# Query and key projections ordered by dimension and then head, so that a stack row is one 16 KB run in DRAM

## What is computed

```
q = _split_heads(query @ Wq.T + bq, B, S)
k = _split_heads(key @ Wk.T + bk, B, S)
v = _split_heads(value @ Wv.T + bv, B, S)
scores = jnp.einsum('bhqd,bhkd->bhqk', q, k) / jnp.sqrt(jnp.float32(D_K))
scores = jnp.where(m == 0, jnp.float32(NEG), scores)
p_attn = jax.nn.softmax(scores, axis=-1)
x = jnp.einsum('bhqk,bhkd->bhqd', p_attn, v)
```

## Time and profile before

| | us |
|---|---|
| median of 3 runs | 1913.74 |
| lowest and highest | 1909.86 and 1918.1 |
| the profiled execution, its own time | 1915.38 |
| its span, first to last instruction | 1913.6 |
| PE busy | 1609.9 (84%) |
| DVE busy | 1219.6 (64%) |
| ACT busy | 1094.1 (57%) |
| POOL busy | 771.6 (40%) |
| mean granted clock of TensorE | 0.929 |

### The profile page before, as it was taken

One profiled execution on the slowest core, in us unless ns is written; L12 is line 12 of the kernel. 1 busy time (PEld: TensorE's weight loads), 2 busy tenths in 40 slices (PEclk: granted clock), 3 DMA queues, 4 the chain that ended last, 5 costly groups with the idle time before them and its releaser, 6 DMA issues.

```text
span 1913.6 us, 34724 instructions
## 1 busy us (share of the span) xinstructions
PE 1609.9 (84%) x10422; PEld 1188.9 (62%) x10422; DVE 1219.6 (64%) x3300; ACT 1094.1 (57%) x2418; POOL 771.6 (40%) x962
## 2 busy tenths in 40 slices
PE   5942778999999899999999889989999899999764
PEld 4731556666666666666666566666666666666542
DVE  5854255676677667766676667666766676676533
ACT  1210235666666666665666666666666566666653
POOL 2335333444444344443444344443444444444221
PEclk9965788999999999998999999999999999999876
DMA  8711333333223212232333332322222233322200
GB/s 269 225 26 44 84 73 73 74 79 80 73 75 79 70 51 72 73 74 71 79 79 80 80 79 79 77 72 65 75 72 62 62 74 79 79 79 63 52 13 11
DMA packets 148988, 147.25 MB, mean 77 GB/s; under 512 B 10930, under 2 KB 147772, under 8 KB 148540
## 3 DMA queue, kind: packets, MB, share of 16 engines
q1 hardware_dynamic: 148796, 144.92, 29.1%
HBM read 99.79 MB, written 42.99 MB: 75 GB/s over the span
## 4 chain that ended last, share of the span: by engine, by line
PE 35%; issue 20%; DVE 14%; DMA 12%; POOL 9%; SPq 6%; ACT 4%; DVEq 0%; POOLq 0%; ACTq 0%
PE bank L1381 15%; DMA qs<-qsplit_d 9%; PE bank L1302 6%; PE bank L1275 4%; PE bank L1264 3%; PE bank L1249 3%; DVE hm L1084 2%; SPq L527 2%; SPq L543 2%; POOL pl L661 2%; DMA qsplit_d<-pl 2%; POOL hid L640 2%; DVE mx L1036 2%; POOL x L656 2%; DVE bn L854 1%
## 5 line engine op out<-in xcount | busy, mean ns | idle before, releaser
L786 ACT ACTIVATE pt<-bank 128x512 f32<-128x512 f32 x512 | 302.2, 590 | 257.4 <-PE bank L1249 257.2
L1036 DVE TENSOR_REDUCE mx<-bank 128x2 f32<-128x512 f32 x512 | 334.6, 683 | 80.4 <-PE bank L1302 80.0
L635 POOL TENSOR_TENSOR x<-x,et 128x256 f32<-128x256 f32 x256 | 190.1, 743 | 329.6 <-ACT et L820 329.4
L1302 PE MATMUL bank<-ks,qs 96*128 96x256 f32 x1024 | 231.6, 311 | 76.2 <-DMA qs<-qsplit_d 59.6
L1302 PEld LDWEIGHTS bank<-ks,qs 96*128 96x128 f32 x1024 | 174.8, 200 | 153.0 <-issue 63.5
L640 POOL TENSOR_TENSOR hid<-hid,t 128x256 f32<-128x256 f32 x256 | 187.1, 731 | 171.9 <-DVE t L1078 168.7
L1249 PE MATMUL bank<-qs,ks 98*128 98x256 f32 x1024 | 237.4, 314 | 13.3 <-ACT pt L786 9.0
L1249 PEld LDWEIGHTS bank<-qs,ks 98*128 98x128 f32 x1024 | 163.5, 198 | 54.7 <-ACT pt L786 25.5
L1381 PE MATMUL bank<-ewh,xah 128*128 128x512 f32 x512 | 184.1, 442 | 10.7 <-issue 10.7
L1078 DVE SCALAR_TENSOR_TENSOR t<-th,bank 128x256 f32<-128x256 f32 x256 | 107.1, 418 | 103.1 <-ACT th L832 95.5
L1006 DVE SCALAR_TENSOR_TENSOR x<-bank,gg,x 128x256 f32<-128x256 f32 x256 | 123.4, 482 | 73.4 <-PE bank L1381 70.3
(11 more groups left out here) (184 smaller groups left out, 3181.0 us busy)
## 6 DMA issues: line engine op xcount, KB each, us to landing
ks<-ksplit_d SPq DMA_DIRECT2D x96, 256.0 KB
qs<-qsplit_d SPq DMA_DIRECT2D x96, 256.0 KB, 5.9
x<-in_x SPq DMA_DIRECT2D x32, 256.0 KB, 3.6
va<-in_ctxT SPq DMA_DIRECT2D x32, 256.0 KB, 3.6
xl<-in_x SPq DMA_DIRECT2D x32, 256.0 KB
ct<-in_ctxT SPq DMA_DIRECT2D x32, 256.0 KB, 2.8
ksplit_d<-ph SPq DMA_DIRECT2D x32, 256.0 KB, 2.2
ksplit_d<-pl SPq DMA_DIRECT2D x32, 256.0 KB, 2.5
```

The source lines that it names most:

```text
L635: pool.tensor_tensor(x3[:, b.quad, t], x3[:, b.quad, t], et[:], ALU.add).then_inc(e_sum[t], 1)
L786: act.activation(pt[:, s % 4].rearrange("p a c -> p (a c)"), cbank[:, :], ACT.Exp).then_inc(ex_made[s % 4], 1)
L1036: dve.tensor_reduce(mx[:, t, 2 * p:2 * p + 2], shared[:].rearrange("p (h s) -> p h s", h=2), AX_X, ALU.max).then_inc(mx_made[t], 1)
L1302: ins = pe.matmul(shared[:, j * S:(j + 1) * S], qs[par][0:QROWS, h, t * P:(t + 1) * P], ks[par][0:QROWS, h, :], start=True, stop=True)
```

## The change

The channels of q and k come out as d*16 + h in place of h*16 + d. For this the columns of the two weights are permuted once in the first stage: Wq and Wk are loaded into `xl`, and ACT copies them, permuted, into `wq` and `wk` (four copies of 128 x 256), when the first stage's other work on ACT is done. The two biases are read from DRAM in the new order, in four DMAs of one column each. The scratch rows are then ordered by dimension and then head, so the 16 rows of one dimension stand one behind another. `v` and Wo are as they were, and so is the content of the stacks.

```diff
+        by_head = [xl[:, i] for i in range(2)]
...
-        N_EARLY, N_RAW, N_W = 3, 5, 11
+        N_EARLY, N_RAW, N_W = 3, 5, 13
...
             eng.wait_ge(w_ld, 16 * N_W)
+            eng.wait_ge(moved, WEIGHTS_MOVED)
...
-            for dst, src in ((wq, wqT), (wk, wkT), (wv, wvT), (wo, woT)):
+            for dst, src in ((by_head[0], wqT), (by_head[1], wkT), (wv, wvT), (wo, woT)):
                 sp.dma_start(dst[:], src.rearrange("(k p) n -> p k n", p=P)).then_inc(w_ld, 16)
             for dst, src in ((bq_c, bq), (bk_c, bk)):
-                sp.dma_start(dst[:], src).then_inc(w_ld, 16)
+                for k in range(KT):
+                    sp.dma_start(dst[:, k:k + 1], bass.AP(src.tensor, k * P // H * KT, [[KT, P // H], [1, KT], [KT * DH, P // DH], [1, 1]]),
+                                 allow_slow_non_contiguous=True).then_inc(w_ld, 16)
...
-                        sp.dma_start(ks[b.par][row:STACK * DH:STACK].bitcast(F32), ksplit_d[b.par, i].rearrange("(h d) s -> d h s", d=DH))\
+                        sp.dma_start(ks[b.par][row:STACK * DH:STACK].bitcast(F32), ksplit_d[b.par, i].rearrange("(d h) s -> d h s", d=DH))\
...
-                        sp.dma_start(qs[b.par][row:STACK * DH:STACK].bitcast(F32), qsplit_d[b.par, i].rearrange("(h d) s -> d h s", d=DH))\
+                        sp.dma_start(qs[b.par][row:STACK * DH:STACK].bitcast(F32), qsplit_d[b.par, i].rearrange("(d h) s -> d h s", d=DH))\
...
-            act.activation(v0[:, 1], maxb[:, 0:NG * P], ACT.Copy).then_inc(v_made, 1)
+            act.activation(v0[:, 1], maxb[:, 0:NG * P], ACT.Copy).then_inc(moved, 1)
...
+            act.wait_ge(w_ld, 16 * N_W)
+            for src, dst in zip(by_head, (wq, wk)):
+                for k in range(KT):
+                    ins = act.activation(dst[:, k].rearrange("p (d h) -> p d h", h=H),
+                                         src[:, k].rearrange("p (h d) -> p d h", d=DH), ACT.Copy)
+            ins.then_inc(moved, 1)
             pipeline_may_start(act)
...
-            pe.wait_ge(v_made, 1)
+            pe.wait_ge(moved, V0_MOVED)
```

More of the change, by code:

```diff
@@ L376, in build @@
         lagstep = sem("lagstep")
-        v_ready, v_made = sem("v_ready"), sem("v_made")
+        v_ready, moved = sem("v_ready"), sem("moved")
+        V0_MOVED, WEIGHTS_MOVED = 1, 2
         lag_dma = sem("lag_dma")
```

## The result

| | before | after |
|---|---|---|
| median, us (4 runs each) | 1914.10 | 1884.78 |
| lowest and highest | 1909.86 and 1918.10 | 1883.08 and 1887.91 |
| the profiled execution, its time and span | 1915.38, 1913.6 | 1887.91, 1886.1 |

The ratio is 0.9849 (95% interval 0.9826 to 0.9872): 1.5% faster, 29 us, where 1.1% and 21 us were forecast.

The account below looks back on a forecast made before the run. The bound was taken as the drain of a full DMA queue that PE awaits: 1915.4 - 15.8 (waits) - 5 (clock) = 1894.6 us profiled, with the median 1.6 us lower, so 1893 us, 1.1% faster; 80% range 1864 to 1922.

Parts of the forecast that it names:

- What bounds the kernel: Stack reads before `max`: a full DMA queue's drain sets their landing; PE waits 27 times, 59.6 us in all.
- The count of packets: Whole page: packets fall from 148988 by 46000, or less if reads are cut to 4 KB.
- 7.6 ns per KB, 0.73 us a batch: Stack reads: what 1 KB packets cost over long runs, taken from loads to 128 partitions; bounds 0 and 4.0 us.
- The 0.5 us estimated from the Trainium skill's port ceiling: Stack reads into partitions 0 to 63: 8 of 16 ports, about 218 GB/s, so at most 7% gained a batch.
- 0.8 of it passes: PE's 27 waits before `max`: of 19.7 us saved, 0.8 is kept for overlapping DMAs, giving 15.8 us.
- the prediction's signs: What would show it: PE's waits before `max` at 1.1 us in the mean where they were 1.9.
- The clock, 5 us: Behind 12 of 23 steady PE waits the clock halves, costing 1.7 us each; fewer such stretches save 5 us.
- I take a third: Halved clock behind PE's waits: 9 of 12 drops may vanish, 15 us, of which a third is counted.
- The rest at nothing: SP's read issue, the writes, ACT's four weight copies and two more bias DMAs: all counted as 0.
- A: Stack reads: destination sets the rate, run length nearly nothing; 1904 to 1914 us, centre 1909; chance 0.27.
- B: Stack reads: fixed packet cost makes them slow; drain 4.0 us shorter, all 27 waits go, 1856 us; chance 0.13.
- C: Stack reads: engines lose their common block and DRAM serves scattered addresses worse; slower, up to 1943 us; chance 0.15.

Follow-up runs that it names:

- the ladder of run lengths: The kernel before with only the stack reads' run length changed from 1 KB: 512 bytes, ratio 1.0162; 4 KB, 0.9908; 16 KB, 0.9852.
- the rows 6 apart: A part's stack rows written 6 partitions apart, not 4: 1862 us against the kernel before (1 KB runs), 1851 us in the changed kernel (16 KB runs).
- the fill: The kernel before with three filling products ahead of PE's wait for the stacks, in three batches of four, no DMA changed: 1896 us, ratio 0.9885.

## Why the prediction was right

- **What bounds the kernel** was right: the drain of a full DMA queue, with PE waiting at its end in 27 batches, and nothing else took its place; the same 27 batches wait in both kernels.
- **The count of packets** was right, 45792 fewer for 46000, each partition one packet.
- **7.6 ns per KB, 0.73 us a batch**, was too large: 0.41 us by the distance, 4.3 ns per KB. The step that failed is carrying the difference between two rows of loads to 128 partitions over to reads that go to 16; the ladder of run lengths gives 5 ns a packet. The 0.5 us estimated from the Trainium skill's port ceiling (SBUF — State Buffer, "Door 1: The DMA port swizzle") lay nearer. That the ceiling is the reason isn't shown: with the rows 6 apart, where by that page more ports are reached, the long runs gained only 0.25 us. The mean rate of the stack reads from 1.6 to 4.0 us behind q's first issue, over the 27 batches, rose from 199 to 218 GB/s as the views count it, by the packets that start in a stretch; with each packet's bytes spread over its time it is 198 and 211, a little under the forecast of 215 to 225.
- **0.8 of it passes** was too careful: PE's waits fell by 59.6 - 48.5 = 11.1 us, which is 27 x 0.41, and the sums over 28 batches leave nothing that was lost on the way. The 15.8 us of the forecast were 11.1. The waits themselves went from 1.82 us (the prediction's signs say 1.9) to 1.41, not to 1.1.
- **The clock, 5 us**, was too small by more than half: 12 stretches became 4 (9 were said to be able to vanish; by the prediction's own rule it is 10, since only the waits of 2.31 and 2.70 us among the 12 stay over 1.40) and 11.9 us went with the halved time. The step that failed is "I take a third". That other engines hold much of the chain in those stretches is refuted by the fill: 15.4 us by the clock, and 14.8 us off the 28 batches with no DMA landing earlier. Two errors of opposite sign, 5 us too much and 7 too little, made the sum look better than its terms; that is luck. Some 4 us of the gain stand in no term.
- **The rest at nothing** held. SP issues a read in 583 ns where it was 617. ACT's copies take 0.63 us each where a copy of `wmix` takes 0.38 (the 0.33 assumed is half of a row of two that overlap), and end long before they are waited for; the bias loads take 0.60 to 0.64 us each on SP for 0.43:

```profile
93.14 1.27 SPq L479 DMA_DIRECT2D bq_c<-in_bq  x2
94.45 1.24 SPq L479 DMA_DIRECT2D bk_c<-in_bk  x2
...
149.17 0.37 SPq L507 DMA_DIRECT2D xl<-in_x  x1
```

```profile
138.61 1.15 ACT L721 ACTIVATE wq<-xl 128x256 f32<-128x256 f32 x2
139.65 1.15 ACT L721 ACTIVATE wk<-xl 128x256 f32<-128x256 f32 x2
```

The pipeline's first DMA goes out at 149.17 where it was 148.82.
- **The rivals.** A (the destination sets the rate and the run length nearly nothing) is half true: the place is the larger lever, 0.89 us against 0.41, but the packets' cost comes on top of it. B asked for 4.0 us a batch, ten times what came. C (reads that lose their common block) didn't show: the rate rose.

## What to carry to other kernels

When a wait for a DMA ends a full queue, count packets per engine and price each at the few nanoseconds that a ladder of run lengths gives; most of the gain is had at 4 KB. Then ask where the rows are written before asking how: moving the same 1 KB packets to other partitions gave more than making them 16 times as long. And price PE's idle time with what the granted clock does behind it; with the rows 6 apart, waits shorter by 20.9 us brought another 22.2 us by the clock. A wait that can't be taken away can be filled by a product whose result nobody needs, as long as the fill ends before the wait would; that gave about 1% here.

## What the hardware showed that was not expected

- The scatter of the kernel before goes with the clock's. In 37 runs of it, timed beside the first eight experiments, from 1897.28 us at a mean granted clock of 0.935 to 1920.01 at 0.925, time and clock go together (correlation -0.87), 15 us for each 0.01 of clock.
- Behind such a wait the clock goes down in some batches and not in others: 1.56 us had a halved stretch at 374, and 2.19 us at 1748 had none. Each stretch is 3.4 us long or a multiple of it.
- Moving the 16 rows of a read from 4 to 6 partitions apart, with the same packets, was worth 2.6% of the kernel; 8 apart was worth 1.4%.
